# A two-layer transformer kernel: where next round's weight splits, its first head's maxima and its norm splits stand in the order of work

## What is computed

```python
x = x + attention(layer_norm(x, g1, b1), layer_norm(x, g1, b1), wq1, wk1, wv1, wo1, bo1)
x = x + attention(layer_norm(x, g2, b2), context, wq2, wk2, wv2, wo2, bo2)
x = x + geglu_ff(layer_norm(x, g3, b3), w_ff1, b_ff1, w_ff2, b_ff2)
# attention: q, k, v = x @ wq, ctx @ wk, ctx @ wv in 16 heads of 64;
#            softmax(q k^T * 64 ** -0.5) v, then @ wo + bo
# geglu_ff:  a, gate = split(x @ w1 + b1); (a * gelu(gate)) @ w2 + b2, inner width 1024
```

## Time and profile before

| what | value |
|---|---|
| median of 3 runs | 2130.04 us (2129.46 to 2131.5) |
| the profiled execution's own time | 2130.59 us |
| its span, first to last instruction | 2128.9 us |
| mean granted clock of TensorE in it | 0.996 |
| DVE, ACT and POOL busy | 75%, 69%, 65% |
| chain of work that ended last | 87% PE, 6% DVE, 2% POOL, 2% ACT |

### The profile page before, as it was taken

The page is one execution under the profiler, slowest core; times in us unless marked ns, Lnnn a source line. Parts: engine busy times, 40 slices in busy tenths (PEclk is TensorE's granted clock), DMA queues, the critical chain, the costliest instruction groups (busy, mean ns, idle before and its releaser), DMA issues.

```text
span 2128.9 us, 58916 instructions
## 1 busy us (share of the span) xinstructions
PE 2075.7 (98%) x25120; PEld 1414.2 (66%) x25120; DVE 1595.6 (75%) x3014; ACT 1474.5 (69%) x1950; POOL 1382.1 (65%) x896
## 2 busy tenths in 40 slices
PE   6999999999999999999999999999999999999999
PEld 2666666685666666678566666667856666667675
DVE  6888887557688888765768888866577888886654
ACT  4888889345488888934558888883465888887442
POOL 6878886464378887745347888784434888776532
PEclk8999999999999999999999999999999999999999
DMA  4322220050332232004032233110503323210120
GB/s 136 81 56 66 67 67 23 21 106 18 81 90 66 57 78 62 27 14 103 26 95 76 66 79 78 39 36 7 100 18 95 86 64 83 67 39 22 29 58 21
DMA packets 132581, 127.82 MB, mean 60 GB/s; under 512 B 81760, under 2 KB 94048, under 8 KB 132320
## 3 DMA queue, kind: packets, MB, share of 16 engines
q1 hardware_dynamic: 132080, 123.66, 23.2%
q10 hardware_dynamic: 240, 0.39, 0.1%
HBM read 55.72 MB, written 4.19 MB: 28 GB/s over the span
## 4 chain that ended last, share of the span: by engine, by line
PE 87%; DVE 6%; POOL 2%; ACT 2%; issue 2%; DMA 1%; SPq 0%; POOLq 0%; DVEq 0%
PE work L1028 10%; PE scores L1052 9%; PE scores L1045 9%; PE scores L937 8%; PE scores L939 8%; PE scores L938 8%; PE work L1074 5%; PE work L1070 5%; PE work L1072 5%; PE work L937 4%; PE work L939 4%; PE work L938 4%; POOL prob L873 2%; DVE minima L1628 1%; DVE prob L1639 1%
## 5 line engine op out<-in xcount | busy, mean ns | idle before, releaser
L873 POOL TENSOR_TENSOR prob<-prob 128x1024 f16<-128x1024 f32 x328 | 711.5, 2185 | 288.7 <-ACT prob L1427 272.3
L1628 DVE TENSOR_REDUCE minima<-work 128x1 f32<-128x512 f32 x1024 | 682.8, 684 | 53.5 <-PE work L1028 47.4
L1426 ACT ACTIVATE prob<-scores 128x1024 f32<-128x1024 f32 x512 | 528.3, 1032 | 86.1 <-PE scores L1052 67.8
L1427 ACT ACTIVATE prob<-scores 128x1024 f16<-128x1024 f32 x512 | 525.3, 1026 | 0.0
L1070 PE MATMUL work<-vals,prob 128*128 128x65 f16 x4096 | 429.4, 192 | 11.5 <-POOL prob L873 10.2
L1070 PEld LDWEIGHTS work<-vals,prob 128*128 128x128 f16 x4096 | 383.1, 99 | 77.3 <-issue 22.2
L1074 PE MATMUL work<-vals,prob 128*128 128x65 f16 x4096 | 430.0, 195 | 0.0
L1072 PE MATMUL work<-vals,prob 128*128 128x64 f16 x4096 | 429.8, 193 | 0.0
L1072 PEld LDWEIGHTS work<-vals,prob 128*128 128x128 f16 x4096 | 380.1, 97 | 52.4
L1028 PE MATMUL work<-ka,qa 128*128 128x512 f16 x1024 | 391.3, 384 | 21.4 <-DVE minima L1628 15.4
L1074 PEld LDWEIGHTS work<-vals,prob 128*128 128x128 f16 x4096 | 380.5, 97 | 0.0
(11 more groups left out here) (174 smaller groups left out, 4150.3 us busy)
## 6 DMA issues: line engine op xcount, KB each, us to landing
qa<-staged_q SPq DMA_DIRECT2D x128, 128.0 KB, 2.3
ka<-staged_k SPq DMA_DIRECT2D x126, 128.0 KB, 2.3
raw_even<-in_pairs SPq DMA_DIRECT2D x32, 384.0 KB, 3.3
raw_odd<-in_pairs SPq DMA_DIRECT2D x32, 384.0 KB, 3.4
raw_odd<-in_pieces SPq DMA_DIRECT2D x20, 512.0 KB, 3.3
raw_even<-in_pieces SPq DMA_DIRECT2D x20, 512.0 KB, 3.2
qb<-staged_q SPq DMA_DIRECT2D x64, 128.0 KB, 2.3
kb<-staged_k SPq DMA_DIRECT2D x63, 128.0 KB, 2.3
```

Source lines behind the costliest of these rows:

```text
L873: pool.tensor_tensor(prob[1][:, slot, :], prob32[:, slot, :], prob[0][:, slot, :], ALU.subtract).then_inc(a.polished, 1)
L1426: act.activation(prob32[:, n % RING, :], source, ACT.Exp)
L1427: act.activation(prob[0][:, n % RING, :], source, ACT.Exp)\
L1628: dve.tensor_reduce(minima[:, t, h:h + 1], out[:, :], AX.X, ALU.max, negate=True)\
```

## The change

Three moves in the order of work; no instruction is added or left out.

- The splits of the next round's S and C weights stood in the last unit at its steps 3 and 7, each ahead of a polish. They now stand behind the last lower half (`low(TILES - 1, ...)`) and before the merge.
- Of the next round's first head six maxima tiles stood beside output tiles 4 to 7 of the feed-forward (2, 2, 1 and 1), and the last two opened unit 0. All eight now stand beside these output tiles, two each, and unit 0 holds the maxima of the second head, one tile a step, and in its last step also the first tile of the next pair. In round 0 all eight now run before unit 0.
- DVE's splits 0 and 1 of the next round's norm stood in feed-forward steps 11 and 12, ahead of `low`. They now stand in steps 10 and 11, behind `low`.

```diff
--- before.py
+++ after.py
@@ -189,16 +189,13 @@
     return tiles
 
 
-AHEAD_TILES = 6
-MAXIMA_OF = {4: range(0, 2), 5: range(2, 4), 6: range(4, 5), 7: range(5, 6)}
-MAXIMA_BY = {4: "max1", 5: "max3", 6: "max4", 7: "max5"}
+MAXIMA_OF = {t: range(2 * (t - HALF), 2 * (t - HALF) + 2) for t in range(HALF, TILES)}
+MAXIMA_BY = {t: f"max{2 * (t - HALF) + 1}" for t in range(HALF, TILES)}
 
 
 def first_peaks():
 
-    own, other = maxima(0, 0), maxima(0, 1)
-    return [own[6] + own[7], other[0], other[1] + other[2], other[3], other[4], other[5] + other[6],
-            other[7], maxima(1, 0)[0]]
+    return maxima(0, 1)[:TILES - 1] + [maxima(0, 1)[TILES - 1] + maxima(1, 0)[0]]
 
 
 def polished(unit):
@@ -259,9 +256,10 @@
             loads[0].append(Step("reload", 0, par, 0, 0))
         loads[6].append(Step("fetch", ("C", pair + 1), par, 0, 0))
     else:
-        if pair + 2 < PAIRS or last:
-            loads[3].append(Step("split", ("S", min(pair + 2, PAIRS)), par, 0, 0))
-        loads[7].append(Step("split", ("C", pair + 1), par, 0, 0))
+        if pair + 2 < PAIRS:
+            loads[3].append(Step("split", ("S", pair + 2), par, 0, 0))
+        if not last:
+            loads[7].append(Step("split", ("C", pair + 1), par, 0, 0))
         if pair < 5:
             loads[7].append(Step("fetch", ("W", pair + 1), par, 0, 0))
     out = [Step("unit", 0, par, head, 0)]
@@ -305,7 +303,7 @@
     for name, part in (("q0", q[:1]), ("k0", k[:1]), ("v0", v[:1]), ("q1 k1", q[1:] + k[1:])):
         out += taken(part) + [mark(name)]
     out += taken(v[1:]) + [Step("split", ("S", 1), 0, 0, 0), mark("v1")]
-    for n, tile in enumerate(maxima(0, 0)[:AHEAD_TILES]):
+    for n, tile in enumerate(maxima(0, 0)):
 
         at = 1 + max(i for i, step in enumerate(tile) if step.kind == "max" and step.step[1] == 0)
         out += tile[:at] + [mark(f"max{n} first")] + tile[at:] + [mark(f"max{n}")]
@@ -314,7 +312,9 @@
     for pair in range(PAIRS):
         out += self_unit(pair, 0) + self_unit(pair, 1)
     par = (PAIRS - 1) % 2
-    out += low(TILES - 1, par, 1, HEADS - 1) + taken([Step("merge", 0, par, 0, 0)]) + [mark("merge0")]
+    out += low(TILES - 1, par, 1, HEADS - 1)
+    out += [Step("split", (kind, PAIRS), par, 0, 0) for kind in "SC"]
+    out += taken([Step("merge", 0, par, 0, 0)]) + [mark("merge0")]
     for s in range(TILES - LAG, TILES):
         out += value(s, par, 1) + [mark(f"value{s}")]
     return out + taken([Step("merge", 1, par, 0, 0)])
@@ -1339,10 +1339,8 @@
                     beside = {}
                     if ahead and t >= HALF:
 
-                        tiles = range(MAXIMA_OF[t].start, MAXIMA_OF[t].stop)
-                        names = [f"max{i}{end}" for i in tiles for end in (" first", "")]
-                        places = (0, 2, 4, 6) if len(tiles) == 2 else (2, 5)
-                        beside = {c: (lambda name=name: ahead(name)) for c, name in zip(places, names)}
+                        names = [f"max{i}{end}" for i in MAXIMA_OF[t] for end in (" first", "")]
+                        beside = {c: (lambda name=name: ahead(name)) for c, name in zip((0, 2, 4, 6), names)}
                     project(index, t, 6, beside=beside)
                     if ahead:
                         for name in marks.get(t, []):
@@ -1835,10 +1833,10 @@
                                              op0=ALU.add, op1=ALU.mult).then_inc(inner_ready, 1)
                     if n < 2:
                         split(index, n + 2)
-                    elif ahead and n in (11, 12):
-                        split(index + 1, n - 11)
                     if n:
                         low(n - 1)
+                    if ahead and n in (10, 11):
+                        split(index + 1, n - 10)
                     if ahead and 2 <= n < 6:
                         if n == 2:
                             hold(dve, next_loaded, (g + 1) * 16)
```

## The result

The changed kernel takes 2118.64 us, the median of 4 runs (2117.57 to 2119.64), against 2130.32 of the kernel before measured with it: a ratio of 0.9945, with a 95% interval of 0.9933 to 0.9957. The forecast was 2118.0 in a range of 2113.5 to 2122.5. The profiled execution took 2118.80 us, span 2117.1, against 2130.59 and 2128.9. Lines L320 to L1340 have the same numbers in both kernels (L873, L937, L1114); those behind are two lower in the changed one (L1626 is L1628 of before). The edits of the experiments shift them by up to three.

A forecast was written before the change was run, and what follows sets the result against it. PE was taken as the bound, with work in 98% of the span, so only its waits and half-clock time could yield. The terms −7.8 − 1.55 − 1.8 − 1.5 + 0.5 = −12.15 gave 2118.0 us, range 2113.5 to 2122.5.

The forecast's parts named there:

- Part 1: End of self-attention, rounds 0 to 2: weight splits behind the last polish gain 2.60 us each, 7.8 in all.
- The cover behind the moved splits: Before PE's turn at the next norm: 0.1 to 1.1 us of slack, costed at nothing, bound 0.5 per round.
- The 1.55 us of clock: End of round 0's attention: the dip to half clock goes with the waits, 1.55 us more gained; other end 0.
- Part 2: Late feed-forward, three transitions: norm splits one step sooner end PE's wait before its first projection, 0.59 us each, 1.8 gained.
- The bound from the contention: Norm split 0 beside POOL's bias in the feed-forward: by the skill's rule it costs 1.53 us again, by its twin 0.68.
- my sum: DVE's feed-forward timing: split 0 at 1.5 us, split 1 ending at 1051.8 to 1052.1, 1.4 us or more ahead.
- Part 3: Three transitions: all eight maxima tiles beside output tiles gain 0.5 us each, 1.5 in all; bounds 1.0 and 0.
- the sum of the two stalls: Unit 0: the tempting claim that both maxima stalls (0.77 and 0.68, each + 0.16) vanish, 1.8 us per transition.
- The chain from the first q projection to k: Unit 0: table load, two exps, q copy and take hold k 6.83 us behind, with no maxima in it.
- The wait for the next pair's DMA: Transitions, second k take to the next pair's arrival: way two maxima shorter, 0 to 0.4 us may be lost.
- The start: Round 0 before unit 0: four more maxima and a later clock rise cost 0.5 us; 1.5 gained if clock rises as before.
- a sum of 12.15: Whole kernel: all terms together, −7.8 − 1.55 − 1.8 − 1.5 + 0.5 = −12.15 us.

The follow-up runs named there:

- E4: The changed kernel with the first scaling of each of the two moved weight splits done three times, a drain between them; 2131.06 us in one run.
- E2: The kernel before with all eight maxima tiles beside output tiles, nothing else; 2129.93 us against 2130.91, ratio 0.9996.
- E3: The kernel before with norm splits 0 and 1 one step sooner, nothing else; 2129.37 us against 2130.91, ratio 0.9995.
- E1: The kernel before with the weight splits alone moved behind the last lower half; 2121.91 us against 2130.91, ratio 0.9959.
- E5: The changed kernel with a 2-column exp on ACT behind its last feed-forward norm copy, loading the exp table early; 2116.92 us, ratio 0.9936 to the kernel before.
- E8: The changed kernel once more, unedited, on the chip of E5 to E7; 2118.73 us, ratio 0.9943 to the kernel before.
- E6: The changed kernel with the order of before in the first unit of round 0 alone; 2118.27 us against 2118.73.
- E7: The changed kernel with the edits of both E5 and E6; 2115.94 us, ratio 0.9931 to the kernel before.

## Why the prediction was right, and where it was not

**Part 1, the weight splits.** Right in size and place: 2.60 us in each of rounds 1 and 2, and 4.18 in round 0 of the profile, where 4.15 was forecast. Round 3 had been a fair picture of the other rounds without their splits. The cover behind the moved splits was put at 0.1 to 1.1 us and is 0.9: both splits ran at their fast length, 7.1 us with the drains. E4 shows that this cover is all there is.

**The 1.55 us of clock inside it was right for this pair of profiles; that its dip fell in the profile of before was luck.** I had it go with its stall. E2 has the stall and no dip; E3 has both. Over the profiles of before, E2 and E3, nine ends of an attention had the 3.4 us of waits and two of them a dip. Six profiles without these waits (E1, the changed kernel, E5 to E8) have 18 such ends and no dip, and E4's three waits of 3.1 us had three. So the dips went with the stalls; what decides whether a stall brings one is not shown. Two of nine would be worth 1.0 us per launch on the mean.

But a profile is one execution, and the mean granted clock on record for each run says more. A launch whose profile has 13.65 us at 1.2 GHz in all shows 0.997, one with 17.1 us in all 0.996, and E4 with 27.3 us 0.994; a dip of 3.4 us takes off 0.0008. The 28 runs of the kernel before that were made beside E1 to E8 show 0.997 in 7, 0.996 in 11 and 0.995 in 10: on the mean 1.1 stretches of 3.4 us beyond the 13.65, some of which may lie in the start. In E2 six of ten runs show 0.994, which is at least two dips if the start has 17.1 us in them as in its profile; these six took 2130.8 us on the mean and the other four 2127.3. With the stalls gone the 13 runs of the changed kernel and E5 all show 0.996, and the 8 of E6 and E7 0.997, which, with the starts of their profiles, leaves no room for a dip. So my estimate for the dips is 1.0 us per launch by the profiles and up to 1.1 x 1.55 = 1.7 by the runs' clocks, and 1.55 lies inside. The Trainium skill ("TensorE: Matmul & The Clock Gate", "What's actually happening") has the monitor out of step with the kernel; that equal stalls dip in one case and not in another agrees with it, and does not prove it.

**Part 2, the norm splits.** Right: 0.59 us three times, and nothing behind it is late. The bound from the contention was needed. DVE in round 1 of the changed kernel, which answers to the earlier trace rows:

```profile
1041.38 1.76 DVE L1671 TENSOR_TENSOR hT<-t,hT 128x512 f16<-128x512 f32 x1
...
1044.74 0.68 DVE L1671 TENSOR_TENSOR hT<-t,hT 128x512 f16<-128x512 f32 x1
```

The first, beside POOL's bias, took 1.76 us, more than the 1.5 of my sum. The Trainium skill ("SBUF — State Buffer", "Who interferes with whom") says that a DVE instruction with two SBUF inputs contends with a POOL instruction that reads SBUF. The trace agrees: 1.76 us in the three splits beside the bias, 0.66 to 0.69 in the 45 others. Split 1 ended at 1045.42 and PE's first projection did not wait.

**Part 3, the maxima.** The net of each transition's terms was right: −0.53 against −0.5, where the sum of the two stalls would have been −1.8. The chain from the first q projection to k was 6.83 us and is 6.70; the projection itself starts 0.87 later by the four maxima ahead of it. E5 takes the table load out of the chain and k follows. The wait for the next pair's DMA that I had bounded at 0.4 did not come in the transitions.

**The start was the term furthest off in the first pair of profiles.** Forecast +0.5, profiled +1.44. A third of that is not the order at all. The first maxima matmul, ahead of which nothing was changed, ends a wait for a DMA, and the DMA came later. Before, and after:

```profile
29.59 0.62 PE L1028 MATMUL work<-ka,qa 128*128 128x512 f16 x1 [5.17 <-DMA kb<-staged_k]
```

```profile
30.07 0.61 PE L1028 MATMUL work<-ka,qa 128*128 128x512 f16 x1 [4.96 <-DMA kb<-staged_k]
```

That is 0.48 us, and 0.95 remain. The clock's later rise fits these, though no run takes it alone: I had it rise just behind the first projection of unit 0, as before (the projection starts at 38.87, the clock rises at 41.64). In the first profile after, the projection starts at 41.83 and the clock rises at 46.46.

By all ten profiles: with the old order (before, E1, E3, E6, E7) the slow stretch was about 13.65 us in four and 17.1 in E1, and the first score of unit 1 came at 62.9 to 64.2, mean 63.6. With the new order (the changed kernel twice, E2, E4, E5) it was 17.1 in all five, and the score came at 63.3 to 65.5, mean 64.4. Counted from the first maxima matmul, which itself comes at 28.8 to 30.6, the means are 34.2 us with the old order and 34.7 with the new: a cost of 0.45, which is near the +0.5 of the forecast. Neither difference is clear of the scatter. E7 against E5 (1.0) and E6 against E8 (0.5) fit both.

The longer slow stretch is clear on the chip of E5 to E8. Besides the five profiles, all 13 runs of the changed kernel and E5 show a mean clock of 0.996, and all 8 of E6 and E7, on the same chip as E5 and E8, 0.997. Of E1's four runs three show 0.996. Why four more maxima ahead of the projection delay the clock's rise, and why it was late in E1 with the old order, is not shown.

**What of the good number was luck.** The profiled pair moved by 11.8 us against a sum of 12.15, and the medians by 11.7 against 12.0. The start took 0.9 us more than its term, and units 2 to 14, put at nothing, gave back 0.4. They differ by up to 0.4 in a round between two profiles of the same kernel (E8), so that help was chance.

## What to carry to other kernels

A round of the same kernel that lacks the work in question is a good price list: laid side by side at a common instruction it gave 2.60 us where the waits alone said 3.4. Work moved out of one queue position stands ahead of something else: find that reader, and give its cover a number. Where a copy engine changes its function table, the load is a link of the first chain behind it; one small instruction of the new function in an idle stretch takes it out. Here that was 0.86 us each time. And one profile is one execution: where the clock dips in some launches only, the mean granted clock of every run counts what a single trace cannot.

## What was not expected of the hardware

A stall of PE of some 3 us costs more than itself, but not each time. In E4 three single waits of 3.1 us were followed each by 3.4 us at 1.2 GHz and cost 4.5 us a round. Three waits that summed to 3.4 us, with work between them, did so at two of nine ends in the profiles, and, as I read the runs' mean clock, at 12 or more of 30 in E2. And at the start the order of four matmuls went with 3.4 us of clock: a slow stretch of 13.65 us in four of five profiles with the old order, 17.1 in five of five with the new.
